# A mixture of experts and three convolution layers on one core: token-stationary gate products, interleaved statistics, bulk loads behind the first gather, later turns back

## The reference

```python
# block 0, on x = gn(x) as (2048, 512):
logits = x @ gate_w.T                      # (2048, 8)
top_logit, top_idx = top_k(logits, 2)
gw = softmax(top_logit)
for e in range(8):                         # F = 1024
    we = sum(where(top_idx == e, gw, 0))
    y = (silu(x @ w1[e].T) * (x @ w3[e].T)) @ w2[e].T
    out = out + we[:, None] * y
# blocks 1 to 3, on gn(x): causal depthwise convolutions with 3, 7 and 15 taps,
# their channels regrouped by head (96 per head) and mixed by w_mix (32 x 96)
x = x + block(gn(x))
```

## Time and profile before

| | |
|---|---|
| median of 3 runs | 1070.13 us (1069.55 to 1070.31) |
| profiled execution, its time | 1071.84 us |
| profiled execution, first to last instruction | 1070.2 us |
| TensorE matmuls busy | 1007.4 us (94%) |
| VectorE / ScalarE / GpSimd busy | 491.7 / 318.3 / 189.5 us |
| mean granted clock of TensorE | 0.969 |

### The profile page before, as it was taken

The page is one execution under the profiler, slowest core; times in us unless marked ns, Lnnn a source line. Parts: engine busy times, 40 slices in busy tenths (PEclk is TensorE's granted clock), DMA queues, the critical chain, the costliest instruction groups (busy, mean ns, idle before and its releaser), DMA issues.

```text
span 1070.2 us, 14224 instructions
## 1 busy us (share of the span) xinstructions
PE 1007.4 (94%) x5089; PEld 842.3 (79%) x5090; DVE 491.7 (46%) x658; ACT 318.3 (30%) x435; POOL 189.5 (18%) x229
## 2 busy tenths in 40 slices
PE   5569999999999999999999999968999999996998
PEld 3267888888888888888888888858888988895787
DVE  4772245146116336116336154156635893588011
ACT  2412244144125234125244144122401230122113
POOL 2030212112111212111212111111400231023100
PEclk9859999999999999999999999979999999998999
DMA  9563115962981894981994985981566367634557
GB/s 397 241 241 136 31 29 191 393 220 81 405 318 29 338 390 137 409 305 28 352 392 138 408 290 230 362 270 60 175 202 192 110 206 209 184 110 138 179 159 213
DMA packets 84864, 238.05 MB, mean 222 GB/s; under 512 B 8544, under 2 KB 50656, under 8 KB 69920
## 3 DMA queue, kind: packets, MB, share of 16 engines
q1 hardware_dynamic: 76608, 214.54, 53.9%
q0 software_dynamic: 8080, 23.07, 9.1%
q10 hardware_dynamic: 144, 0.02, 0.0%
HBM read 129.86 MB, written 111.94 MB: 226 GB/s over the span
## 4 chain that ended last, share of the span: by engine, by line
PE 69%; DMA 12%; DVE 10%; issue 3%; SPq 3%; ACT 2%; POOL 0%; DVEq 0%; ACTq 0%; POOLq 0%
PE gate_ps L965 13%; PE up_ps L965 13%; DMA w_raw<-in_w13T 10%; PE y_ps L952 9%; PE head_ps L1481 7%; PE head_ps L1485 7%; PE head_ps L1482 7%; PE y_ps L955 4%; SPq L442 3%; PE hT_ps L974 2%; DVE scaled L1275 1%; DVE split L1285 1%; PE xT_ps L942 1%; PE xT_ps L883 1%; PE head_ps L1493 1%
## 5 line engine op out<-in xcount | busy, mean ns | idle before, releaser
L1481 PE MATMUL head_ps<-split,ring 128*128 128x256 f32 (+1 forms) x525 | 182.6, 348 | 1.1 <-ACT split L1170 1.0
L965 PE MATMUL gate_ps<-front 128*128 128x512 f32 x560 | 177.3, 398 | 2.3 <-DVE xT_lo L819 1.4
L1485 PE MATMUL head_ps<-split,ring 128*128 128x256 f32 (+1 forms) x525 | 178.3, 340 | 1.1 <-DVE split L1285 1.0
L1482 PE MATMUL head_ps<-split,ring 128*128 128x256 f32 (+1 forms) x525 | 177.5, 338 | 0.0
L965 PE MATMUL up_ps<-front 128*128 128x512 f32 x560 | 173.6, 392 | 0.0
L834 DVE TENSOR_TENSOR hidden<-silu,up_ps 128x1024 f32<-128x1024 f32 x35 | 42.7, 1221 | 239.1 <-ACT silu L620 239.1
L965 PEld LDWEIGHTS up_ps<-front 128*128 128x128 f32 x560 | 105.8, 189 | 22.3
L965 PEld LDWEIGHTS gate_ps<-front 128*128 128x128 f32 x560 | 103.0, 190 | 23.5 <-DVE front L783 2.1
L620 ACT ACTIVATE silu<-gate_ps 128x1024 f32<-128x1024 f32 x35 | 35.9, 1024 | 270.5 <-PE up_ps L965 270.5
L952 PE MATMUL y_ps<-w_hi,hT_hi 128*128 128x512 f32 x280 | 112.4, 401 | 1.2 <-ACT hT_hi L602 1.2
L1485 PEld LDWEIGHTS head_ps<-split,ring 128*128 128x128 f32 x525 | 100.4, 191 | 13.4 <-DVE split L1285 1.7
(11 more groups left out here) (187 smaller groups left out, 1286.1 us busy)
## 6 DMA issues: line engine op xcount, KB each, us to landing
filters<-rows SPq DMA_DIRECT2D x56, 1568.0 KB, 18.4
w_raw<-in_w13T SPq DMA_DIRECT2D x32, 1024.0 KB, 6.4
w_raw<-in_w2T SPq DMA_DIRECT2D x16, 1024.0 KB, 6.2
ring<-filters SPq DMA_DIRECT2D x15, 1024.0 KB, 6.3
ring<-filters SPq DMA_DIRECT2D x18, 640.0 KB, 4.7
ring<-filters SPq DMA_DIRECT2D x18, 512.0 KB, 4.4
ring<-filters SPq DMA_DIRECT2D x33, 256.0 KB, 3.3
ring<-filters SPq DMA_DIRECT2D x96, 64.0 KB, 4.8
```

Of the source, the lines that this page charges most:

```text
L965: last = nc.tensor.matmul(o[:, n, :], a[:, k, :], b[:, k, t, n * 512:(n + 1) * 512], start=(k == 0 and a is xT_hi and b is w13_hi), stop=( ...
L1481: nc.tensor.matmul(place, kernel_hi, x_hi, start=(u == 0 and a == 0), stop=False)
L1482: nc.tensor.matmul(place, kernel_lo, x_hi, start=False, stop=False)
L1485: nc.tensor.matmul(place, kernel_hi, x_lo, start=False, stop=False)
```

## The change

Seven edits, in the order of the program.

- Gate products: 128 tokens are now the stationary operand and the gate's 8 columns the moving one, 16 products per batch, accumulated straight into the logits' bank. Copy and transposes of the logits go.
- Statistics: VectorE takes the sums of batch b in two halves between the steps of batches b - 1 and b - 2; TensorE's and ScalarE's programs are reordered to match.
- The picks' weights are computed after the row numbers have been taken; ScalarE splits two chunks of w1/w3 before the exponential.
- The first gather takes its row numbers straight from `from_row`; the clearing of the filters' buffer stands ahead of it.
- SP issues taps, mix and half of w2 when the logits are done, and the other half after the first gather has landed; the copy of x to `acc` is issued after the second gather has landed.
- The weights' products are done within the first block, after the transposes of the second block's rows.
- Layers: ScalarE splits piece 2 before it takes piece 3, and turns back begin with task 7 of the last layer instead of task 5.

```diff
@@ sync
-            sp.wait_ge(weight_block_ok, PARTS_OF_WEIGHT * TOP_K)
-            for half in range(2):
-                load_w2(sp, 0, half)
             sp.wait_ge(normal_out, 16 * BATCH)
+            sp.wait_ge(logits, BATCH)
             sp.dma_start(taps_sb, taps).then_inc(taps_in, 16)
             sp.dma_start(mix_sb, mixT).then_inc(taps_in, 16)
+            load_w2(sp, 0, 1)
+            sp.wait_ge(row_in, 16)
+            sp.wait_ge(weight_block_ok, PARTS_OF_WEIGHT * TOP_K)
+            load_w2(sp, 0, 0)
@@ gpsimd
-            pool.wait_ge(x_in[BATCH - 1], 16)
-            pool.dma_start(acc[0:TOKENS, :]...).then_inc(acc_ready, 16)
-            pool.dma_start(acc[TOKENS:TOKENS + P, :], pad_row).then_inc(added, 16)
...
             def add_block(g):
+                pool.wait_ge(acc_ready, 16)
...
             pool.wait_ge(normal_out, 16 * BATCH)
+            pool.wait_ge(logits, BATCH)
+            nc.gpsimd.memset(filter_sb, 0.0).then_inc(filter_zero, 1)
             pool.wait_ge(route_ok, 1)
-            fetch_rows(0)
-            nc.gpsimd.memset(filter_sb, 0.0).then_inc(filter_zero, 1)
+            gather(from_row[:, 0:1])
             pool.wait_ge(xT_done, 1)
             fetch_rows(1)
-            pool.wait_ge(values_ok, 1)
-            pool.wait_ge(acc_ready, 16)
+            pool.wait_ge(row_in, 32)
+            pool.dma_start(acc[0:TOKENS, :]...).then_inc(acc_ready, 16)
+            pool.dma_start(acc[TOKENS:TOKENS + P, :], pad_row).then_inc(added, 16)
@@ scalar
+            root(0)
             for b in range(BATCH):
-                root(b)
-                if b:
-                    copy_logits_T(b - 1)
-                copy_gate_xT(b)
-            copy_logits_T(BATCH - 1)
+                copy_gate_xT(b, range(KD - 1))
+                if b + 1 < BATCH:
+                    root(b + 1)
+                copy_gate_xT(b, [KD - 1])
+            split_w13(0, 0, range(2))
             act.wait_ge(gap_ready, 1)
             nc.scalar.activation(best[:, 3, :], best[:, 2, :], ACT.Exp).then_inc(exped, 1)
...
+            split_w13(0, 0, range(2, KD))
             act.wait_ge(table_ready, 1)
-            split_w13(0, 0)
@@ vector
-            for b in range(BATCH):
-                lane_statistics(b)
-                deviation(b)
-                variance(b)
-                normalise(b)
+            lane_sums(0, early)
+            lane_sums(0, late)
+            lane_averages(0)
+            lane_sums(1, early)
+            deviation(0)
+            lane_sums(1, late)
+            lane_averages(1)
+            for b in range(2, BATCH):
+                variance(b - 2)
+                lane_sums(b, early)
+                normalise(b - 2)
+                deviation(b - 1)
+                lane_sums(b, late)
+                lane_averages(b)
+            variance(BATCH - 2)
+            normalise(BATCH - 2)
+            deviation(BATCH - 1)
+            variance(BATCH - 1)
+            normalise(BATCH - 1)
...
                 xT_low(g + 1)
+                if isinstance(g, int):
+                    take_weights()
-            expand_weights()
-            take_ids()
-            split_w13(0, 0, [0])
-            take_targets()
-            take_weights()
-            split_w13(0, 0, [1, 2])
-            xT_low(0)
-            split_w13(0, 0, [3])
+            take_ids()
+            take_targets()
+            weigh_picks()
+            split_w13(0, 0, [0])
+            xT_low(0)
+            split_w13(0, 0, [1, 2, 3])
+            expand_weights()
             take_pair_end()
@@ tensor
-                for k in chunks:
-                    pe.wait_ge(gxT_sb, KD * b + k + 1)
-                    last = nc.tensor.matmul(xT_ps[0:E, :], gate_sb[:, k, :], gate_xT[:, b % 2, k, :],
-                                            start=(k == 0), stop=(k == KD - 1))
+                for k in range(KD):
+                    pe.wait_ge(gxT_sb, KD * b + k + 1)
+                    for q in range(QUARTERS):
+                        i = b * QUARTERS + q
+                        last = nc.tensor.matmul(logits_bank(b)[:, i * E:(i + 1) * E], gate_xT[:, b % 2, k, q * P:(q + 1) * P], gate_sb[:, k, :],
+                                                start=(k == 0 and q == 0), stop=(k == KD - 1 and q == QUARTERS - 1), skip_group_check=True)
                 last.then_inc(logits, 1)
...
-            for b in range(BATCH):
-                transpose_batch(b)
...
+            group_means(1)
             pe.wait_ge(gate_in, 16)
+            for b in range(BATCH - 1):
+                transpose_batch(b, range(KD // 2))
+                group_deviation(b + 1)
+                transpose_batch(b, range(KD // 2, KD))
+                if b + 2 < BATCH:
+                    group_means(b + 2)
+                gate_product(b)
+            transpose_batch(BATCH - 1, range(KD))
+            gate_product(BATCH - 1)
...
                 next_rows(g + 1)
-                if not isinstance(g, int):
+                if isinstance(g, int):
+                    find_weights(0)
+                    find_weights(1).then_inc(values_done, 1)
+                else:
                     down(g - 1, 2 * e if first else 2 * e + 2)
@@ layers, scalar
-                if i + 1 < HALVES:
+                if i + 1 < HALVES and i != 2:
                     take_stream(i + 1)
                 high(0, i)
+                if i == 2:
+                    take_stream(i + 1)
@@ layers, tensor, between(n, u)
                 if l == LAYERS - 1:
-                    if u == 1 and k >= 9:
+                    if u == 1 and k >= 12:
                         unturn(n - 2)
-                    elif k < 9 and 2 * k + u >= 12:
-                        unturn(n - k + (2 * k + u - 12))
+                    elif 7 <= k < 12:
+                        unturn(n - k + 2 * (k - 7) + u - 1)
```

More of the change, by code:

```diff
@@ L488, in _, with gather @@
             nc.gpsimd.memset(restart[:, :, 0:1], 0.0).then_inc(consts, 1)
-            pool.wait_ge(x_in[BATCH - 1], 16)
-            pool.dma_start(acc[0:TOKENS, :].rearrange("(p a) n -> p (a n)", p=P),
-                           x.rearrange("b (p a) h w -> (b p) (a h w)", a=TOKENS // P)).then_inc(acc_ready, 16)
-            pool.dma_start(acc[TOKENS:TOKENS + P, :], pad_row).then_inc(added, 16)
+            def gather(row):
+                pool.indirect_dma_start(
+                    out=block_row[:, :], out_offset=None, in_=normal,
+                    in_offset=bass.IndirectOffsetOnAxis(row.bitcast(u32), 0)).then_inc(row_in, 16)
             def fetch_rows(g):
@@ L499, in fetch_rows @@
                 nc.gpsimd.tensor_copy(fetch[:, :], from_row[:, at]).then_inc(fetch_ok, 1)
[L500 to L503, removed]
+                wait_apart(pool, fetch_ok, g, passed)
+                gather(fetch[:, 0:1])
             def add_block(g):
+                pool.wait_ge(acc_ready, 16)
                 wait_apart(pool, added, 16 * (g + 1), y_free)
@@ L547, in root, with copy_gate_xT, split_w13 @@
                 nc.scalar.activation(rstd[:, b, 1:2], rstd[:, b, 0:1], ACT.Sqrt).then_inc(rooted, 1)
[L549 to L552, removed]
+            def copy_gate_xT(b, chunks):
+                if b >= 2 and 0 in chunks:
+                    act.wait_ge(logits, b - 1)
+                for k in chunks:
                     act.wait_ge(gxT_ps, KD * b + k + 1)
                     nc.scalar.activation(gate_xT[:, b % 2, k, :], gate_banks[k], ACT.Copy).then_inc(gxT_sb, 1)
[L556 to L572 removed]
+            def split_w13(e, g0, chunks=range(KD)):
+                for k in chunks:
                     act.wait_ge(w13_in[k], 16 * (e + 1))
@@ L577, in split_w13 @@
                     nc.scalar.activation(w13_hi[:, k], w13_raw[:, k], ACT.Copy).then_inc(w13_hi_ok, 1)
+            root(0)
+            for b in range(BATCH):
+                copy_gate_xT(b, range(KD - 1))
[3 more added lines that the diff above has]
+            split_w13(0, 0, range(2))
+            act.wait_ge(gap_ready, 1)
+            nc.scalar.activation(best[:, 3, :], best[:, 2, :], ACT.Exp).then_inc(exped, 1)
             def split_w2(e, g0):
@@ L648, in count, with lane_sums, lane_averages @@
                 ins.then_inc(d_step, 1)
-            def lane_statistics(b):
+            def lane_sums(b, quarters):
                 dve.wait_ge(x_in[b], 16)
-                for q in range(QUARTERS):
+                for q in quarters:
                     count(nc.vector.bn_stats(bn[:, b, q, :], rows[:, b * QUARTERS + q, 0:D]))
+            def lane_averages(b):
                 flush()
@@ L674, in _ @@
             dve.sem_inc(filters_out, FILTERS_FREE)
-            for b in range(BATCH):
-                lane_statistics(b)
-                deviation(b)
-                variance(b)
-                normalise(b)
+            early, late = range(QUARTERS // 2), range(QUARTERS // 2, QUARTERS)
+            lane_sums(0, early)
[17 more added lines that the diff above has]
+            normalise(BATCH - 1)
```

(7 more changed lines are left out.)

49 lines of the change are left out of this document (11 added, 38 removed).

## The result

The changed kernel takes 1066.13 us (median of 13 runs, 1058.55 to 1068.56), the kernel before 1071.01 (13 runs, 1069.55 to 1072.62): ratio 0.994, 95% interval 0.992 to 0.9961. The forecast was 1064.4. The profiled execution took 1066.55 us, its span is 1064.9 and the mean granted clock 0.962.

A forecast was written before the change was run, and what follows sets the result against it. TensorE, busy 94% of the span, was taken as the bound, so lateness before its first product stays; -10.7 - 0.5 + 10.0 - 7.1 + 2.6 = -5.7, applied to the 1070.13 median, gave 1064.4 us, range 1050 to 1069.

The forecast's parts named there:

- Later turns: Last layer: without TensorE's wait for ScalarE, 8.85 us idle and 1.8 of half clock go; -10.7, ends -7.0 and -11.5.
- Third take: First layer: ScalarE splits piece 2 before taking turn 3, shortening TensorE's 0.69 us wait; -0.5, ends 0 and -1.2.
- Statistics: Gate stage: half a batch's bn_stats run inside each VectorE wait, so VectorE stops being the bound; TensorE starts +2.5 us later.
- Gate products: Gate stage: 32 weight-load-bound instructions per batch, two of four groups at high clock; +10.0 (start's +2.5 within), ends -2.8 and +17.0.
- Rival 1: Gate stage: clock stays up through the gate products, or loads don't slow with it; gate -2.8, total 1051.6; chance 0.22.
- Rival 2: Gate stage: the clock never comes up; gate +17.0, total 1071.4, no change to measure; chance 0.10.
- Rival 3: Gate stage: load and product don't overlap, 0.35 us per instruction at the low clock; total 1088; chance 0.05.
- rival 4: Last layer: the later turns fail and TensorE meets the same wait at task 8; +8.85, total 1073.3; chance 0.03.
- To the first product: From logits to first product: weighing moved -0.3, first gather issued earlier -2.8, landing sooner -4.0; sum -7.1.
- The term of 2.28 for the copy: Before the first gather: GpSimd's copy of 2.28 us goes, part of the gather's earlier issue, taken as -2.8.
- First block: First block: weights' products +1.6 and a possible clock drop +1.0; +2.6, ends +1.5 and +6.
- the +1.0 for a drop of the clock: First block: bare loads of the weights' products may drop the clock; one drop costs some 1.8, counted as +1.0.

The follow-up runs named there:

- e1: The kernel before with only the later turns back (from task 7 of the last layer): 1060.37 us, ratio 0.990.
- e11: The changed kernel again, unedited, one profiled run to see where its clock falls in the gate stage: 1062.76 us.
- e3: The changed kernel with the old gate products, copy and transposes of logits, but the new statistics: 1053.33 us, ratio 0.9832.
- e5: The changed kernel with an unread 512-column product behind every second gate product: median 1090.53 us, ratio 1.0194; profiled execution 1083.75.
- e6: e3 with taps, mix and half of w2 issued when the row numbers are done, beside the first gather: 1055.86 us, ratio 0.9851.
- e7: e3 with GpSimd again copying the row numbers before the first gather and VectorE splitting w1/w3 right behind them: 1053.99 us, ratio 0.9835.
- e9: The kernel with old gate products, new statistics and weights' products in two waits, plus unread dense products in four TensorE waits: 1054.8 us, ratio 0.9833.
- e4: The changed kernel with the new gate products but the old statistics, one batch after the other: 1065.52 us, ratio 0.9954.
- e10: e9 with row numbers taken before the weights' first half is expanded, and 7 dense products ahead of the weights' products: 1053.18 us, ratio 0.9831.

## Why the prediction was right, step by step

**Later turns (-10.7).** Right. e1, which has nothing else, measured -10.8. In its profile the layers are 12.0 shorter, 1.3 of which arose in the first layer, where the kernel before has a fall of the clock near 735 that e1 lacks. The changed kernel's layers are 10.28 shorter, with a wait of 1.2 us in them that e1 does not show.

**Third take (-0.5).** No run has it alone. The first layer's second set of shared windows comes 25.36 us behind the layers' start in the kernel before and 25.35 in e1, which have the old order, and after 24.41 in the changed kernel and 24.87 in e11: 0.5 to 0.95.

**Statistics (+2.5 at the start, no longer the bound).** The start was right: rows ready at 14.7, forecast 15.2. That VectorE stops being the bound was right too (5.9 to 6.3 us a batch in e3), but it is worth only 0.4 in the time, as the later start takes it back.

**Gate products (+10.0).** The load sets the pace, and the clock sets the load: shown (0.109 and 0.213 to 0.218 each). "Two of the four groups at the high clock" was right for e11 (stage end 50.9) and one too many for the first profile (54.2); the forecast of 52.9 lies between the two. The reasoning named a cause that e5's profiled execution bears out: dense products between the loads are all that was added there, and the clock stayed up. What failed is the choice of one pattern for a quantity that differs from run to run, and the forecast says nothing of the spread (10 us against 3). Rival 1, the clock stays up, would have needed e3's end of 42 us and did not come in either profile; the fastest of 13 runs, 1058.55, does not reach its 1051.6. Rival 2, the clock never rises, came in neither profile, but it can't be shut out for all runs: two of the 13 (1067.66 and 1067.71) have a mean clock of 0.993 against 0.962 in the profile, which would itself have 0.992 if its first 100 us read 1.00. As the column shows 1.00 until the first fall, the clock may have been low there from the start; no trace of these two was kept. Their time is 3.7 below rival 2's 1071.4. Rival 3 is out by the 0.213 per instruction, rival 4 by the end of the wait of the earlier trace rows.

The rule of the Trainium skill that I set against the trace (TensorE: Matmul & The Clock Gate, LDWEIGHTS) gives an estimate of 3.4 us a group at either clock; e11 has 3.72 and 6.97 in one execution, so the measurement decides against it at the low clock.

**To the first product (-7.1).** Right in sum (-7.65) and in its two large terms: issue -3.0 (forecast -2.8), landing -4.4 (-4.0). TensorE did not wait for the rows of the third gather. e6 shows that the landing is a matter of what moves beside the gather, as argued. The term of 2.28 for the copy was right in size, but it was read as the copy's own; it was the split's hold on GpSimd (e7), and it went because the new order of VectorE's work takes the split away from the gather, as much as because the copy went.

**First block (+2.6).** The +1.6 for the weights was 0.96, and the +1.0 for a drop of the clock did not come: 3.57 us of bare loads behind dense products left it at 1.00. That no drop follows there, while e9 had one, is the term I would size anew; the earlier trace rows had shown only the absence of a rise. This error (-1.6) and that of the gate stage (+1.35) cancel, and the gate stage's own size differs by 3.3 us between the two profiles. That the sum came within 0.4 of the forecast (-5.3 against -5.7) is partly luck.

**What is open.** The new wait for the filters in the last layer (1.2; 1.7 in e11, 1.8 in e4) stands in three of the four profiles with the new gate products, not in e5's, and in none with the old ones at that place (e9 and e10 have one of 0.9 and 1.2 near 858 us). It is worth 1 to 2 us, may be part of the 11.6 that the gate products cost, and was not explained. Nor is it known what sets the moment at which the clock falls or rises in the gate stage.

## What to carry to other kernels

When a product's moving side is narrow, count its weight loads and not its columns, and give the sum at both clocks, as one program went at either here; the new form turned 8 dense instructions per batch into 32 loads and cost 11.6 of the 17.8 us that the rest gave. A part that is "beside other work" should be tried alone, as bundles hide a loser: without its gate products the change measured 1053.3, and with the weights in two waits 1051.4. A start that is late while the clock is still down costs less than it shows, as part of the time at half clock goes (e7), and what is filled in to raise the clock can move the delay to an engine that has no such reserve (e9).

## What the runs showed of the hardware

- One program, the same instructions: groups of 32 loads took 3.72, 4.08, 6.83 or 6.97 us according to the clock, and which groups differed between two executions.
- Two GpSimd instructions that read row numbers from SBUF and started within a VectorE operation on two SBUF inputs waited for its end: a copy took 2.27 instead of 0.18, a gather's issue 2.25 instead of 0.99 to 1.18. A plain DMA issue within such operations took 0.58.
- A gather of 128 rows landed after 3.44 us alone and 7.33 with 3 loads beside it.
- In e9 unread dense products began at 45.67 and the clock was up from 50.7 on; bare loads began at 54.94, and it was down from 57.6 on although four dense products had followed them.
- In the changed kernel the clock fell at 21.9 with TensorE busy without a gap; 32 bare loads behind dense products (95.21 to 98.78) left it up.
